# Where the edge indices, the one-hots' columns and the edge products live in a two-layer graph kernel

## The reference

```python
# layer 0: two SAGE convolutions over the same edges
agg  = segment_sum(x[src], dst, n)
cnt  = segment_sum(ones, dst, n)
h    = relu(agg / max(cnt, 1) @ W1_l.T + b1_l + x @ W1_r.T)
agg2 = segment_sum(h[src], dst, n)
x    = layernorm(x + agg2 / max(cnt, 1) @ W2_l.T + b2_l + h @ W2_r.T)
# layer 1: edge attention with 4 heads of 16
Q, K, V = x @ Wq.T + bq, x @ Wk.T + bk, x @ Wv.T + bv
Ee    = edge_attr @ We.T + be                       # one row of 64 for each edge
score = (K[src] * Q[dst] / sqrt(16) * Ee).reshape(-1, 4, 16).sum(-1)
score = exp(clip(score, -5, 5))
out   = segment_sum(V[src] * score[..., None], dst, n)
x     = layernorm(x + out)
```

## Time and profile before

| what | us |
|---|---|
| median of 3 runs | 12531.65 (12527.64 to 12540.04) |
| the profiled execution, its own time | 12490.73 |
| its span, first to last instruction | 12488.9 |
| first gather to last, first sums | 3956.7 |
| the same, second sums | 3957.7 |
| the same, attention | 4120.4 |
| all the rest (start, dense stages, output) | 454.1 |

### The profile page before, as it was taken

How to read it: one execution, slowest core, us unless ns; L and a number is a source line. 1 busy time by engine, 2 the same in 40 slices (tenths; PEclk the granted TensorE clock), 3 DMA queues, 4 the chain that set the end, 5 groups by cost and what they waited for, 6 DMA issues and landing times.

```text
span 12488.9 us, 169430 instructions
## 1 busy us (share of the span) xinstructions
PE 4731.8 (38%) x37310; PEld 3932.7 (31%) x37311; DVE 4654.1 (37%) x10192; ACT 1542.6 (12%) x3498; POOL 9179.7 (74%) x9383
## 2 busy tenths in 40 slices
PE   1111111111112311111111111277777777777776
PEld 0011111111111200011111111166666667667776
DVE  3222222233333322222222222354445555555555
ACT  0000000000000100000000000033333333333333
POOL 5777777777777577777777777737777777777776
PEclk9999999999999999999999999997777777877777
DMA  2111111111111111111111111112222222222222
GB/s 59 40 40 40 40 40 40 40 40 40 39 40 38 44 40 40 39 40 40 40 40 40 39 39 39 37 53 74 75 75 75 75 75 77 76 76 75 76 75 71
DMA packets 716290, 649.53 MB, mean 52 GB/s; under 512 B 470247, under 2 KB 566151, under 8 KB 716152
## 3 DMA queue, kind: packets, MB, share of 16 engines
q0 software_dynamic: 300000, 512.60, 16.1%
q1 hardware_dynamic: 416277, 136.79, 4.8%
HBM read 629.36 MB, written 19.26 MB: 52 GB/s over the span
## 4 chain that ended last, share of the span: by engine, by line
POOL 68%; issue 27%; PE 2%; DVE 1%; DMA 0%; POOLq 0%; ACT 0%; DVEq 0%; SPq 0%; ACTq 0%
POOL rows L334 46%; POOL kv L334 22%; PE ps_q L387 1%; PE ps_t L381 0%; PE ps_kv L402 0%; POOLq L328 0%; DMA node_h<-in_dst 0%; ACT stageT L518 0%; PE ps_t L395 0%; POOLq L180 0%; PE ps_e L402 0%; ACT stageT L527 0%; DMA kv<-kv_rows,edge_ids 0%; DMA edge_ids<-in_edges 0%; PE ps_sum L445 0%
## 5 line engine op out<-in xcount | busy, mean ns | idle before, releaser
L334 POOL DMA_INDIRECT kv<-kv_rows,edge_ids x3125 | 3168.4, 1014 | 1155.3 <-issue 949.6
L372 PE MATMUL ps_sum<-rows,hot 128*128 128x193 bf16 x7220 | 1397.3, 359 | 6585.1 <-DMA rows<-h_rows,edge_ids 2770.0
L334 POOL DMA_INDIRECT rows<-h_rows,edge_ids x3125 | 3005.6, 962 | 1049.4 <-issue 952.1
L334 POOL DMA_INDIRECT rows<-x_rows,edge_ids x3125 | 3004.7, 961 | 1038.1 <-issue 952.0
L372 PEld LDWEIGHTS ps_sum<-rows,hot 128*128 128x128 bf16 x7220 | 850.9, 132 | 7131.2 <-issue 7087.2
L693 DVE SCALAR_TENSOR_TENSOR hot<-edge_ids,base,iota 128x640 bf16<-128x640 int32 x2071 | 1835.2, 886 | 1312.7 <-issue 1300.3
L713 DVE TENSOR_REDUCE part_sum<-ps_sum 128x64 f32<-128x192 f32 x1444 | 516.7, 358 | 4272.3 <-PE ps_sum L372 4272.3
L445 PE MATMUL ps_sum<-message,node_h 128*128 128x64 f32 x6260 | 1054.0, 330 | 19.5 <-DVE message L819 10.2
L445 PEld LDWEIGHTS ps_sum<-message,node_h 128*128 128x128 f32 x6260 | 988.8, 243 | 51.0 <-DVE message L819 48.5
L515 ACT ACT_TABLE_LOAD x14 | 18.0, 1283 | 4051.0 <-DVE node_x L724 4050.8
L810 DVE TENSOR_TENSOR kq<-kv,ps_q 128x320 f32<-128x320 f32 x375 | 182.9, 488 | 897.0 <-DMA kv<-kv_rows,edge_ids 728.3
(11 more groups left out here) (152 smaller groups left out, 5827.0 us busy)
## 6 DMA issues: line engine op xcount, KB each, us to landing
attr<-in_edge_attr SPq DMA_DIRECT2D x627, 160.0 KB
rows<-x_rows,edge_ids POOLq DMA_INDIRECT x3125, 2.4
rows<-h_rows,edge_ids POOLq DMA_INDIRECT x3125, 2.4
kv<-kv_rows,edge_ids POOLq DMA_INDIRECT x3125
edge_ids<-in_edges SPq DMA_DIRECT2D x1877, 5.0 KB, 1.6
kv_rows<-node_h SPq DMA_DIRECT2D x14, 448.0 KB, 3.0
x_rows<-node_q SPq DMA_DIRECT2D x14, 336.0 KB, 2.6
h_rows<-node_q SPq DMA_DIRECT2D x14, 336.0 KB, 2.6
```

Source lines behind the costliest of these rows:

```text
L334: nc.gpsimd.indirect_dma_start(out=into[:, u, k, 0:width], out_offset=None, in_=table_rows, in_offset=bass.IndirectOffsetOnAxis(ap=edge_id ...
L372: mm = nc.tensor.matmul(ps_sum[:, 0:ROW + 1], hot[:, 0, k, :], rows[:, u, k, 0:ROW + 1], start=(k == 0), stop=(k == K - 1))
```

## The change

Five things are changed together.

1. **Sources in a ring.** `src_ids` holds the source indices of 25 groups, loaded 5 groups at a time (SP, 128x5x5). GpSimd waits for such a load once in 5 groups, and for `group_done` itself before each group. Its loop now runs over 25 rings of 25 groups instead of 125 turns of 5.
2. **Resident destinations.** `dst_ids` holds the destinations of all groups; they are loaded in the first stage, 50 groups at the start, then 25 at a time.
3. **One-hots a group ahead** in the sums: `hot` has a slot for each group and the next group's one-hot is made ahead of the wait for this group's sum. Extra one-hots and sums have their own semaphores and their own PSUM bank.
4. **Edge products made in the sums.** The attributes are loaded, transposed and multiplied by We during the first sums (3 of a turn's 5 groups) and the second (2 of 5); ScalarE copies the product out and stores it in DRAM (`ee_rows`). Attention loads the products (160 KB a group, as the attributes were) and has no attribute transposes and products.
5. **Columns, weights and kq in PSUM.** `columns` (f32), `weight` and `kq` are parts of `ps_t`. The products come to VectorE from SBUF (`ee_in`), where they came from PSUM before.

To make room, `rows` now lies over `kv`, `w_in` over `stage`. The core of the diff:

```diff
-                        pool.wait_ge(p.ids[u], t * 16 + 16)
-                        hold(pool)
+                with pool.Fori(0, BIG) as T:
+                    for j in range(SUBS):
+                        pool.wait_ge(ids_in, T * (16 * SUBS) + 16 * (phase * TURNS + j + 1))
+                        for u in range(SLOTS):
+                            at = j * SLOTS + u
+                            pool.wait_ge(p.group_done, T * RING + at + 1)
+                            hold(pool)
...
-                                in_offset=bass.IndirectOffsetOnAxis(ap=edge_ids[:, u, k:k + 1], axis=0),
+                                    in_offset=bass.IndirectOffsetOnAxis(ap=src_ids[:, at, k:k + 1], axis=0),
...
+        columns = ps_t[:, 896:1024]
+        weight = ps_t[:, 0:K * HEADS]
+        kq = ps_t[:, 64:64 + K * D].rearrange("p (k f) -> p k f", k=K)
...
-                v.scalar_tensor_tensor(into, edge_ids[:, u, K:2 * K].rearrange("p (k o) -> p k o", o=1).to_broadcast([P, K, P]),
-                                       base[:, bass.ds(b, 1)], iota[:].rearrange("p (o n) -> p o n", o=1).to_broadcast([P, K, P]),
+                v.scalar_tensor_tensor(into, dst_ids[:, bass.ds(g * K, K)].rearrange("p (k o) -> p k o", o=1).to_broadcast([P, K, P]),
+                                       base[:, bass.ds(b, 1)], columns.rearrange("p (o n) -> p o n", o=1).to_broadcast([P, K, P]),
...
-                s.link(v.tensor_tensor(kq[:], kv[:, u, :, 0:D], ps_query[u % 2][:, 0:K * D].rearrange("p (k f) -> p k f", k=K), ALU.mult))
-                v.tensor_tensor(kqe[:], kq[:], ps_edge[u % 2][:, 0:K * D].rearrange("p (k f) -> p k f", k=K), ALU.mult).then_inc(p.scored, 1)
+                s.link(v.tensor_tensor(kq, kv[:, u, :, 0:D], ps_query[u][:, 0:K * D].rearrange("p (k f) -> p k f", k=K), ALU.mult))
+                v.tensor_tensor(kqe[:], ee_in[:, u], kq, ALU.mult).then_inc(p.scored, 1)
...
+                        sum_group(ps_main[u], hot[:, u], u, p.summed)
...
+                        e = first_e + t * per + u
+                        if 0 < u <= per:
+                            edge_products(e - 1)
+                        if u < per:
+                            turn_attr(u, e, (phase * TURNS) * 16 + t * 16 + 16)
...
+                        nc.scalar.copy(ee_out[:, i, :], ps_e[:, 0:K * D]).then_inc(ee_ready, 1)
+                        act.wait_ge(ee_ready, e + 2)
+                        nc.scalar.dma_start(ee_v[:, bass.ds(e, 1), :].rearrange("p a c -> p (a c)"), ee_out[:, i, :]).then_inc(ee_stored[i], 16)
```

More of the change, by code:

```diff
@@ L35 @@
 CH = 7
+SUBS = 5
+EE_A, EE_B = 3, 2
+AHEAD = 2
 EPS = 1e-5
@@ L299, in _ @@
+                with sp.Fori(TURNS - SUBS + 1, TURNS) as t:
+                    products(t)
             sp.wait_ge(be_stored, 16)
@@ new lines, in sum_turn @@
+            def sum_turn(p, t, nodes, count_edges):
+                words = group_words(ENG.DVE, t, 0, SLOTS + 1)
+                for u in range(SLOTS):
+                    before, first, more = words[u]
+                    g = t * SLOTS + u
+                    one_hot(g + 1, block_at(words[u + 1][1]), hot[:, (u + 1) % SLOTS], p.hot)
+                    dve.wait_ge(p.added, g + 2)
+                    dve.wait_ge(p.summed, g + 1)
+                    add_rows(block_at(first), ps_main[u], nodes, count_edges, p.step, g + 1, p.added)
+                    with dve.If(more):
+                        dve.wait_ge(p.added, g + 3)
+                        hold(dve)
+                        with dve.Fori(0, more) as j:
+                            n = before + j
+                            b = block_at(first + j + 1)
+                            one_hot(g, b, hotT[:], p.x_hot)
+                            dve.wait_ge(p.x_summed, n + 1)
+                            add_rows(b, ps_extra, nodes, count_edges, p.x_step, n + 1, p.x_added)
+                            dve.wait_ge(p.x_added, n + 2)
+                            hold(dve)
+                    v.engine_nop().then_inc(p.group_done, 1)
```

329 lines of the change are left out of this document (198 added, 131 removed).

## The result

The changed kernel takes **12181.77 us** (median of 4 runs, 12160.21 to 12182.09), the kernel before 12532.94 us beside it (4 runs, 12527.64 to 12540.04). The ratio is 0.9715, 95% interval 0.9698 to 0.9732, so 351 us fewer.

The account below looks back on a forecast made before the run. GpSimd's gathers were taken to bound the kernel, some lengthened by VectorE operations. The profiled 12490.7 us less 321, other terms 0, gave 12169; from the runs' median, 12531.65 less 321 gave 12210 us, range 12190 to 12305.

Parts of the forecast that it names:

- The holds, -321 us: VectorE operations with two SBUF inputs delay gathers started under them; PSUM inputs for one-hots and messages gain 321 us.
- The block additions: VectorE additions (L716) keeping two SBUF inputs; could delay gathers by 139 us at most, taken as 0.
- Loop starts, register operation and kinds of wait, 0: GpSimd's new ring loop, extra register operation and direct wait cost 0; upper bound 94 us.
- Rival C: Each GpSimd group pays a second 0.30 us pause for register operation and waits, adding 563 us: 12773 us; chance 3%.
- the loop part of B: GpSimd's 75 new loop starts give back part of the gain, up to 94 us; chance of the whole rival 11%.
- D: Another engine paces the sums through waits between TensorE, ScalarE and stores: between 12305 and 12500 us; chance 2%.
- Start, +0 to 5: SyncE's new loads ahead of the x_rows stores delay the first gather by 0, at most 5 us.
- Edge products in the sums, 0 for the chain: Moved edge work costs the chain 0; TensorE's busy time rises some 680 us in first sums, 450 in second.
- Ring, resident destinations, one-hots ahead, 0: GpSimd's source ring, resident destinations and earlier one-hots in the sums each change the time by 0.
- GpSimd again: What limits the changed kernel next: GpSimd's gathers at 1.249 us each, 11706 us of the new span.
- Rival A, 8%: Gathers stay delayed because the one-hot's scalar from SBUF or its SBUF write is responsible: 12505 or 12532 us; chance 8%.
- From the profiled execution to the median: Whole kernel: the runs' median stays 40.9 us above the profiled execution after the change, giving 12210 us from 12169.

Follow-up runs that it names:

- the mask: One more register operation per decoded word on TensorE, ScalarE and VectorE, values unchanged; on chip 9 the kernel before takes 12585.43 us, the changed kernel 12158.52 us.
- the masked kernel before: Kernel before plus one register operation per decoded word on TensorE, ScalarE and VectorE: 12585.43 us on chip 9, ratio 1.0071.
- the masked changed kernel: Changed kernel plus one register operation per decoded word on TensorE, ScalarE and VectorE: 12158.52 us on chip 9; ratio 0.9694 on chip 0.

## Why the prediction was right, and where it was not

**The holds, -321 us: right, 9 us too small.** Profiled against profiled the gain is 330.5. The 4.4 us kept back for the gather at 97.37 belonged to a queued one-hot and went too. The other 4 to 5 us are the median: gathers that nothing holds average 943.5 ns, not the 944 from which the 329 were counted. The 3.0 us beside the bias addition stayed (now 3.71 us, 2.8 too long). The block additions, taken at 0, hold 14 gathers for 0.6 us together.

**Loop starts, register operation and kinds of wait, 0: right.** None of the 9372 pauses within a stage exceeds 0.316 us. Rival C (563 us) and the loop part of B (up to 94 us) didn't happen. D didn't either: GpSimd waits for nobody.

**Start, +0 to 5: right.** The first gather starts at 88.9 instead of 87.88, +1 us; on the other chips with the mask 88.1 and 88.4. The dense gap is 95.97 us instead of 97.26.

**Edge products in the sums, 0 for the chain: right, though by more than I had room for.** TensorE's busy time rose by 797 and 542 us in the sums where I wrote 680 and 450. In the first sums a group's transposes take 0.82 us and its products 1.45, where the earlier trace rows have 0.67 and 0.83; the granted clock is 0.55 there and 0.76 over the attention of the earlier trace rows. The sums' own matmuls did not get longer (680 us, before 698). So the lower clock goes with the difference; that it is all of it isn't shown. TensorE is busy 38% of the stretch.

**Ring, resident destinations, one-hots ahead, 0: not contradicted.** The kernel with both inputs in PSUM leaves at most 38 us for them and the moved products, and has a wait of its own in it; the subtraction from the kernel with the columns alone leaves about nothing. "GpSimd again" as what is late next is right for the changed kernel: no other pause remains in its stages.

**Rival A, 8%:** refuted twice, by the columns alone and by the whole (`base` is still in SBUF).

**From the profiled execution to the median: this step failed.** "The runs' median is 40.9 us above the profiled one; carried over" made 12169 into 12210. It took one distance, between one execution and three others, for a property of the kernel that the change wouldn't touch. After the change the distance is 21.6 us, and these 19 us and the 9 above are the 28 us by which the forecast was off. With 12181.77 below the low end of 12190, the range was too narrow at the side where I had taken only the spread of the runs.

What the distance consists of shows in the runs of the changed kernel. It has two levels of time: 12158 to 12160 (all five runs on chip 9 lie within 0.9 us) and 12182 (four runs within 0.6 us). The profile on chip 12 fell on the upper level, that on chip 9 on the lower; the gathers' line of the latter stands first:

```profile
L422 POOL DMA_INDIRECT kv<-kv_rows,src_ids x3125: 940/944/961, 8192.0 to 12091.7; - x196
```

and on chip 12:

```profile
L422 POOL DMA_INDIRECT kv<-kv_rows,src_ids x3125: 941/947/962, 8208.0 to 12115.2; - x196
```

From first to last start these are 3899.7 and 3907.3 us for 3124 steps, 1.2483 and 1.2507 us, 7.6 us for one stage and some 23 for three. In the run of the result the profiled execution was of the lower level and the three others of the upper one (12181.5 to 12182.09), which is its 21.6 us. That this level also lay in the 40.9 us of the kernel before is likely, but not shown: its runs of the same comparison, 12532.94, are 33 and 39 us above those on chips 9 and 12 (12499.46 and 12493.9), where the changed kernel's lie at 12158. If it did, 19 us are left, and where they come from stays open. Holds that its runs had and the profiled execution hadn't would be one source: its runs spread over 22 to 27 us on one chip where those of the changed kernel keep to 1 at one level, and the mask showed how much a small edit moves the holds. Unprofiled runs leave no trace, so nothing shows it, and one figure speaks against it. I had put the question to the kernel with the columns alone: its median should lie 22 us above its profiled execution if unprofiled runs have more holds, and 42 if the distance is the kernel's own. It lies 13 us above. With over 400 us of holds the distance is 9 us (the masked kernel before, chip 9) and 6 us (weight alone), so it doesn't grow with the holds. The 19 us are also no more than chips and runs differ by: the 23 runs of the kernel before on chips 9, 10 and 12 lie between 12485.8 and 12515.8 us. What sets the two levels stays open.

## What to carry to other kernels

Where indirect DMAs on GpSimd are the chain, look at the spread of their durations and not at the median alone; if long ones end a fixed time after VectorE operations, count the tensor inputs of these in SBUF, and move one to PSUM, a constant before anything else (the columns alone gave 2.4% of the 2.85% here). Price such interference as a range: in four kernels with the same one-hots it cost from 332 to 628 us, so one profiled execution doesn't give its size in a neighbouring kernel, nor the distance of the runs from it. And when a reduced kernel comes out slower than the whole change, look first for a wait that only the reduced one has, as the 447 us behind ScalarE here.

## What the runs showed of the hardware that I had not expected

**The granted clock of TensorE.** In the kernel before the sums run at a granted clock of 1.00, the 2.4 GHz level, and so they do with the columns in PSUM and nothing else, and with columns and weight there. In the changed kernel it falls within the first sums' beginning; stretches of that kernel, columns as above:

```profile
88.00:100.00 12.00, 0.00 (x0) 0.00 (x0) 10.10 (x13) 1.28 (x1) 8.68 (x9) 1.00 0.37 53
100.00:120.00 20.00, 9.41 (x50) 8.42 (x50) 9.70 (x19) 2.71 (x6) 15.13 (x17) 0.83 0.33 81
120.00:200.00 80.00, 28.46 (x138) 23.67 (x138) 19.73 (x52) 10.10 (x17) 60.49 (x65) 0.52 0.29 69
```

TensorE had stood idle at a granted clock of 1.00, then began on sums and edge products, busy 36% of the last stretch above, and from then on was granted about half, the 1.2 GHz level, through both sums (0.55 and 0.53) and attention (0.50, before 0.76). It costs nothing here, as TensorE isn't on the chain. Nor does all work grow by it. The dense stage's matmuls, in a gap where the clock was 1.00 before and is 0.50 now (before, then after):

```profile
L387 PE MATMUL ps_q<-w,stageT 128*128 128x64 f32 x392 | 91.0, 425 | 27.9 <-ACT stageT L518 27.9
```

```profile
L508 PE MATMUL ps_q<-w,stageT 128*128 128x64 f32 x392 | 91.1, 425 | 27.9 <-ACT stageT L625 27.9
```

They take 425 ns either way. The message matmuls in attention, mean ns before and after, don't:

```profile
L445 PE MATMUL ps_sum<-message,node_h 128*128 128x64 f32 x6260 | 1054.0, 330 | 19.5 <-DVE message L819 10.2
```

```profile
L553 PE MATMUL ps_sum<-message,node_h 128*128 128x64 f32 x6260 | 1466.8, 421 | 0.3 <-DVE message L968 0.3
```

The kernel with both inputs in PSUM keeps its 1.00 in the sums without the edge products there, which speaks for them as the cause; whether they alone bring the clock down wasn't tried.

**Register operations of VectorE and SyncE** of up to 1.4 us on two of the five numbered chips, 0.05 at most on the others. The kernel before takes 15.7 to 16.0 ms there instead of 12.5. That the register operations are all of it isn't shown: in the masked changed kernel on chip 0 VectorE also stands without any record for more than 5 us at a time, 570 times, on chip 9 four times.

**An operation that only waits in VectorE's queue** already holds a gather: by 4.4 us in the kernel before and four others, by 5.65 us in the changed kernel with its columns back in SBUF, each time behind the same memset.
